# Second x tile's load held until three quarters of Wq have landed, three small inputs loaded from ScalarE's queue

## The reference

```python
q = rms_norm((x @ Wq) per head of 64, q_g)[..., :32]
kv = x @ Wkv                       # 1024 -> 128
k, v = rms_norm((kv @ Wk) per head of 32, k_g), kv @ Wv
probs = softmax(causal(q k^T / 8))
x = layernorm(x + pad(probs @ v) @ Wo)
x = layernorm(x + bitlinear(silu(bitlinear(x, w_gate)) * bitlinear(x, w_up), w_down))
```

## Time and profile before

| | us |
|---|---|
| median of 3 runs | 1583.39 (1582.47 to 1631.66) |
| the profiled execution | 1582.16 |
| span of its slowest core (core 2) | 1580.6 |
| spans of all cores | 1572.6 to 1580.6 |
| PE busy | 1278.2 (81%) |
| ACT busy | 824.8 (52%) |
| DVE busy | 804.4 (51%) |

### The profile page before, as it was taken

The page is one execution under the profiler, slowest core; times in us unless marked ns, Lnnn a source line. Parts: engine busy times, 40 slices in busy tenths (PEclk is TensorE's granted clock), DMA queues, the critical chain, the costliest instruction groups (busy, mean ns, idle before and its releaser), DMA issues.

```text
span 1580.6 us, 22883 instructions; the slowest of 8 cores (1572.6 to 1580.6 us)
## 1 busy us (share of the span) xinstructions
PE 1278.2 (81%) x7455; PEld 436.5 (28%) x7494; DVE 804.4 (51%) x1158; ACT 824.8 (52%) x998; POOL 320.9 (20%) x350
## 2 busy tenths in 40 slices
PE   2566676578668589888976989899987999999997
PEld 0221122122112122222221222222222444444443
DVE  2327875457627676423465143415334887273753
ACT  2577565678697467657744668676860121020200
POOL 1024412121220122330203301313032102020320
PEclk9976587559556799899996999899997999999999
DMA  9995866678778687623325423353316888586773
GB/s 248 291 277 149 226 228 212 145 229 267 245 236 228 203 242 222 154 77 107 94 94 154 126 80 96 98 142 108 94 60 173 280 228 220 187 201 229 192 195 130
DMA packets 146513, 283.06 MB, mean 179 GB/s; under 512 B 91744, under 2 KB 92000, under 8 KB 133088
## 3 DMA queue, kind: packets, MB, share of 16 engines
q1 hardware_dynamic: 144816, 272.70, 57.6%
q0 software_dynamic: 1584, 8.91, 3.6%
HBM read 235.96 MB, written 33.55 MB: 171 GB/s over the span
## 4 chain that ended last, share of the span: by engine, by line
PE 58%; DVE 16%; issue 11%; ACT 9%; DMA 4%; POOL 2%; DVEq 0%; SPq 0%; ACTq 0%; POOLq 0%
PE ps_w L1000 16%; PE ps_w L1123 7%; PE ps_sc L1000 7%; PE ps_sc L829 6%; ACT PT L842 6%; PE ps_den L784 4%; PE ps_sc L1123 4%; PE ps_pv L795 3%; DVE S L777 3%; PE ps_w L547 2%; DVE qb L382 2%; PE ps_den L1000 2%; PE ps_pv L1000 2%; PE ps_w L716 1%; ACT R L370 1%
## 5 line engine op out<-in xcount | busy, mean ns | idle before, releaser
L842 ACT ACTIVATE PT<-ps_sc,negM 128x1024 bf16<-128x1024 f32 (+3 forms) x640 | 592.7, 983 | 196.8 <-PE ps_sc L829 194.3
L1000 PE MATMUL ps_w<-R,S 128*128 128x512 fp8e4 x1096 | 294.0, 394 | 29.8 <-DVE R L1019 16.9
L829 PE MATMUL ps_sc<-qn,khat 32*128 32x512 bf16 (+3 forms) x1280 | 200.0, 395 | 77.5 <-ACT PT L842 63.1
L850 POOL TENSOR_TENSOR PT<-PT,tri 128x512 bf16<-128x512 bf16 x64 | 80.0, 1250 | 533.3 <-ACT PT L842 531.5
L784 PE MATMUL ps_den<-PT,ones 128*32 128x512 bf16 (+3 forms) x1280 | 131.6, 401 | 16.7 <-DVE S L773 8.6
L1000 PEld LDWEIGHTS ps_w<-R,S 128*128 128x128 bf16 x1096 | 88.4, 99 | 183.7 <-issue 115.7
L855 POOL TENSOR_SCALAR PT<-PT,hflag_sb 128x512 bf16<-128x512 bf16 x64 | 112.7, 1762 | 109.7 <-ACT PT L842 109.6
L795 PE MATMUL ps_pv<-PT,vtok 128*32 128x512 bf16 (+3 forms) x1280 | 130.4, 398 | 0.2 <-DVE pvb L775 0.2
L1123 PE MATMUL ps_w<-R 128*128 128x512 fp8e4 x416 | 114.7, 402 | 14.5 <-DMA R<-R 11.4
L829 PEld LDWEIGHTS ps_sc<-qn,khat 32*128 32x128 bf16 x1280 | 52.5, 93 | 255.7 <-issue 252.0
L1019 DVE SCALAR_TENSOR_TENSOR R<-R,ps_w 128x512 f32<-128x512 f32 x80 | 54.8, 685 | 130.6 <-ACT R L1013 130.6
(11 more groups left out here) (200 smaller groups left out, 1493.0 us busy)
## 6 DMA issues: line engine op xcount, KB each, us to landing
R<-wffn SPq DMA_DIRECT2D x69, 1024.0 KB, 7.7
R<-scr_w SPq DMA_DIRECT2D x128, 512.0 KB, 4.5
wb<-scr_w SPq DMA_DIRECT2D x64, 512.0 KB, 4.9
scr_w<-qb SPq DMA_DIRECT2D x48, 256.0 KB, 6.5
khat<-wffn SPq DMA_DIRECT2D x9, 1024.0 KB, 14.0
vtok<-wffn SPq DMA_DIRECT2D x9, 1024.0 KB, 7.6
R<-xt POOLq DMA_DIRECT2D x7, 1024.0 KB, 12.8
R<-scr_x SPq DMA_DIRECT2D x12, 512.0 KB, 6.6
```

The costliest lines, as they stand in the source:

```text
L829: t = pe(lambda e, j=j, gi=gi, tc=tc, kc=kc, stc=stc: e.matmul(ps_sc[:, j * 512 + stc:j * 512 + 512], khat[32 * j:32 * j + 32, kc:kc + 128 ...
L842: t = act(lambda e, hf=hf, pp=pp, stc=stc: e.activation(PTr[pp][:, 2 * hf:2 * hf + 2, stc:512], PSr[:, 2 * hf:2 * hf + 2, stc:512], AF.Exp ...
L850: t = pool(lambda e, pp=pp, stc=stc: e.tensor_tensor(PTr[pp][:, :, stc:stc + 128], PTr[pp][:, :, stc:stc + 128], tri.rearrange("p (r n) -> ...
L1000: t = pe(lambda e, c=c, b=b, kw=kk[w], i=i: e.matmul(wring.bufs[b], xqT[u % 2][:, i * 1024 + c * 128:i * 1024 + c * 128 + 128], wbuf[kw][: ...
```

## The change

The three small inputs are issued from ACT's queue in place of SP's. The load of x tile 1 is no longer issued before `latent(0)`, but where the second job begins (after `latent(0)` and the first stage of the first `keys_values` in the lists), and GpSimd's issue of it waits until the third quarter of Wq has landed. Nothing is computed in another way.

```diff
-        dma("sync", gcol[:], dgc, qS)
-        dma("sync", grow, dgr, qS)
-        t_small = dma("sync", hflag[:], dhf, qS)
+        dma("scalar", gcol[:], dgc, qS)
+        dma("scalar", grow, dgr, qS)
+        t_small = dma("scalar", hflag[:], dhf, qS)
...
-        def load_x(c5):
-            t_x[c5] = dma("gpsimd", xt[c5 % 2], dx[c5], qXc[c5 % 2], [xt_free[c5 % 2]])
+        def load_x(c5, after=()):
+            t_x[c5] = dma("gpsimd", xt[c5 % 2], dx[c5], qXc[c5 % 2],
+                          [xt_free[c5 % 2]] + list(after))
...
-        load_x(1)
         latent(0)
...
         for n, job in enumerate(jobs):
+            if n == 1:
+                load_x(1, [t_ld[("wq", 2, 0)]])
             if n == 4:
                 stream_until("wq", 3)
             next(job)
```

## The result

The changed kernel took 1587.07 us in the median of 11 runs, the kernel before 1582.13 us in the median of 11 on the same chips. Medians are of all executions; the ratios leave out those in which cores of one die ran at a lower granted clock and took some per cent longer. The forecast was +4.8 us. The amount was right; the step that the forecast held decisive was not.

What follows compares the result with a forecast made beforehand. The prediction took a mostly TensorE chain, tied to loads only at the start, to bound the kernel. +4.75 + 0 + 0 on 1582.2 gave 1587.0 us for the profiled execution, 1588.2 for the median; range 1581.0 to 1592.0.

Steps and rivals of the forecast that it cites:

- the step that the forecast held decisive: Before the first matmul: late small inputs hold DVE's first instruction and the x casts behind it, 4.75 us later.
- What bounds the start: At the first matmul: two waits end together, x tile 0's cast at 18.95 us and wv's landing at 18.9.
- One packet from each queue in turn, whatever the size: In the first loads: each of the 16 DMA engines takes one packet from either queue in turn.
- Small inputs decide, +4.75: At the start: hflag lands at 20.5 us, tiny operations and casts follow, first matmul at 23.95 against 19.20.
- The assumed lead of SP's queue: In the first loads: SP's x packets get about 2.6 turns done by 3 us, before wkv's packets arrive.
- The weights, +3.0: In GpSimd's first loads: eight more 8 KB packets per engine beside the weights, wv lands at 21.9 us, not 18.9.
- rival 1: At the first matmul: weights decide and small inputs don't, +3.0 us, 1586.4 us; chance 0.26.
- The signs that were named: At the start: DVE's first instruction near 20 us, first matmul near 24; under the weights-decide case, below 15 and at 22.
- The bracket of +3.0 to +7: At the first matmul: +3.0 us if small packets go unhindered, +7 if all 24 turns run at x tile 0's pace.
- Load of x tile 1 moved, 0: On GpSimd's queue: holding this load costs 0; it lands near 39 us, read by PE near 67.
- Carried to the end: After the first matmul: its gain or loss lasts to the end, unless some later wait has slack.
- Rival 2, faster: At the start: everything moves up by SP's 1.39 us, -1.4 to -2 us in all, 1581.8 us; chance 0.20.

Runs made afterwards that it cites:

- e6: Changed kernel with wkv, wk, wv as float32 on ACT's queue ahead of the small inputs, tiny operations later, first matmuls waiting for wkv alone; no ratio, first matmul 15.76 us.
- e2: Changed kernel with the three small inputs back on SP's queue, so only x tile 1's load is held back; ratio 0.9991 to the kernel before.
- e10: Changed kernel with float32 weights ahead of x tile 0 on SP, tiny operations later, first matmuls waiting for wkv alone, x tile 1 at once; ratio 1.0034.
- e12: e9 with the first eight matmuls waiting for wkv alone and x tile 1's load issued at once; ratio 0.9985 to the kernel before.
- e3: Changed kernel, but SP's first x load also waits until the three small inputs have landed; ratio 0.9996 to the kernel before.
- e11: e9 with the first eight matmuls waiting for wkv alone and x tile 1's load held as in the change; 1577.93 us, ratio 0.9974.
- e9: Kernel before with small inputs on SP behind both x tile 0 halves and the tiny operations behind the first eviction; ratio 0.9989.

## Why the prediction was right, and where it was not

- *What bounds the start.* Right. Two waits ended together at 19 us, and `wv` was the hidden one. With x tile 0 3 to 4 us sooner the first matmul came 4.9 us later in the mean.
- *One packet from each queue in turn, whatever the size.* Right, for three queues too (23, 21, 23), and for two hardware queues (e6), of which the trace of before had no row. By the Trainium skill ("DMA: Bandwidth & Descriptors", Queues, rings and completion order) an engine takes a packet of typically 9 to 17 descriptors at a turn. The counts here are of one row's packet against one, and `hflag` was not early.
- *Small inputs decide, +4.75.* This step failed. It put `hflag` at 20.5, behind which the casts would end at 23.7; `hflag` landed at 17.2, and the casts were done at 20.4. The assumed lead of SP's queue, 2.6 turns before GpSimd's packets begin, is the mis-sized term. From 2 to 7 us SP moved 10 + 31 + 24 + 23 + 31 = 119 packets, 7.4 turns, and ACT's queue 162, 10.1 turns, since GpSimd's queue was silent until 7 us. With a lead of 10.1 turns at the prediction's 0.53 us a turn, `hflag` comes 5.4 us ahead of `wv` by this estimate; it came 5.6 ahead (17.2 and 22.8), where the prediction had 1.4.
- *The weights, +3.0.* The decisive term, rival 1 in the prediction, and too small: 22.8 in place of 21.9. I had let GpSimd's packets start at 3 us as before and go slower. They start some 4 us later, and from there to `wv` they take 15.8 us, about what they took before (3 to 18.9), for two things cancel: eight 8 KB packets more beside them, and the two nearly idle microseconds of before, from 3 to 5 (22 packets of GpSimd's), gone. Weights at +3.9 and small inputs at about +1.5 (casts at 20.4 and 18.95) took the places of +3.0 and +4.75. That the sum came out is luck in part, and twice over. The forecast was for core 2, where the first matmul came 3.67 us later and not 4.75; the mean of the cores moved by 4.9 because core 2 had been the latest of the eight before (19.20, mean 17.96), and after the change it was not (22.87, mean 22.83). The signs that were named fell between forecast and rival 1: DVE's first instruction at 17.30 (near 20, or below 15), the first matmul at 22.87 (near 24, or 22). The bracket of +3.0 to +7 held.
- *Load of x tile 1 moved, 0.* Right, by e2, to within its interval of 3 us. The reason given (it stood behind `wv`) fits e10, where it doesn't and costs 6.2 us. It landed at 25.79 + 14.8 = 40.6, 1.6 after the estimate and 28 before its reader (68.55). That its packets out of Wq's way are cover for a sooner start fits e12, where the next load comes late.
- *Carried to the end.* Right: attention starts 5.0 us later, the time is 5.9 longer.
- *Rival 2, faster.* It did not come. SP's 1.39 us were saved (x tile 0 is issued at 1.06 in place of 2.45), and the first matmul came 4.9 later, because the issues that went away had held the x packets back; e3, which holds them back again, is at 18.89. The Trainium skill (same page, Issuing engines are not separate DMA queues) says that issuing on several engines saves only the issue time. The trace agrees with the saving, and shows that the new order can cost more than it.

## What to carry to other kernels

Before a small load is moved to another queue, ask what it stood in front of, and what its own packets and those of the other queues will take turns with: each row of a transfer is a turn, and a tiny row waits as long as a large one of the neighbour. Loads that end a common wait (here x tile 0, `wkv`, `wk`, `wv`) gain only together; give each consumer a semaphore for what it needs, and put tiny operations on late inputs behind the first big ones. Hold a large prefetch back above all when nothing else stands ahead of it in its queue: there it was worth 6 us at the first matmul, in the kernel before at most 3 us of the time, and behind the sooner start of e11 likely 1 to 2.

## What was not expected of the hardware

- GpSimd's first packets came between 3 and 4 us when only tiny packets were in front (before, e3), and from 7 us on when 8 KB packets of SP's were (the change, e9), though GpSimd issued at 1.55 or 1.56 us in all four. The runs show the delay, some 4 us, and not its cause.
- The company of the weights decides: 24 packets on each engine were through by 8.8 us beside tiny packets (e3), by 16.5 beside x tile 0 and then tiny ones (e9), by 22.8 beside x tile 0 and Wq (the change).
